# A two-layer decoder megakernel on one core: weight preparation reordered, one row chunk made full, keys moved to VectorE, a new instruction order

## What is computed

```python
x = _layernorm(x + _L0_attn_ref(x, ...))          # l0: 16 heads, rotary latents of 32, causal softmax
x = _layernorm(x + _L0_xattn_ref(ctx, x, ...))    # x0: q @ (k^T v), no softmax, own norm inside
x = _layernorm(x + _L0_ffn_ref(x, ...))           # f0: 256 -> 704 -> 256, FP4 blocks of 16, silu(gate) * up
x = _layernorm(x + _L1_attn_ref(x, ...))          # l1: causal softmax plus a second, softmax-free branch
x = _layernorm(x + _L1_xattn_ref(x, ctx, ...))    # x1: masked cross attention, then 256 -> 1024 -> 256
x = _layernorm(x + _L1_ffn_ref(x, ...))           # f1: 256 -> 256, FP6 blocks of 32
```

## Time and profile before

| | us |
|---|---|
| median of 3 runs | 1065.53 |
| lowest, highest | 1062.94, 1068.25 |
| the profiled execution, its own time | 1070.73 |
| span of its instructions | 1068.9 |

### The profile page before, as it was taken

The page is one execution under the profiler, slowest core; times in us unless marked ns, Lnnn a source line. Parts: engine busy times, 40 slices in busy tenths (PEclk is TensorE's granted clock), DMA queues, the critical chain, the costliest instruction groups (busy, mean ns, idle before and its releaser), DMA issues.

```text
span 1068.9 us, 29911 instructions
## 1 busy us (share of the span) xinstructions
PE 896.8 (84%) x12078; PEld 692.8 (65%) x12078; DVE 742.0 (69%) x1804; ACT 641.6 (60%) x1867; POOL 348.1 (33%) x604
## 2 busy tenths in 40 slices
PE   2665688999999898989999999999998989887853
PEld 2444466777767676767676776767776766665643
DVE  4956384869686876868686868687777878674342
ACT  1244457586767667585848675766767585836341
POOL 2752121333242323333243423242323333322121
PEclk7868899999999999999999999999999999988776
DMA  9102000000100100010101010000001000000000
GB/s 339 67 2 84 14 2 22 2 14 7 32 5 6 31 2 24 2 29 2 28 3 28 3 27 3 7 24 2 20 2 42 6 8 9 8 6 6 6 6 6
DMA packets 24440, 24.90 MB, mean 23 GB/s; under 512 B 2304, under 2 KB 22640, under 8 KB 24176
## 3 DMA queue, kind: packets, MB, share of 16 engines
q1 hardware_dynamic: 24304, 22.98, 6.9%
HBM read 18.80 MB, written 2.10 MB: 20 GB/s over the span
## 4 chain that ended last, share of the span: by engine, by line
PE 47%; DVE 19%; ACT 15%; DMA 8%; POOL 5%; issue 4%; SPq 2%; DVEq 0%; POOLq 0%; ACTq 0%
PE bank L1175 26%; PE s_tile L1175 13%; DMA out<-x_ 5%; ACT probT L648 5%; PE bank L1287 4%; ACT prob L710 3%; PE bank L1376 3%; POOL rstd L563 3%; DVE rope_ L964 2%; ACT x_ L757 2%; DVE stats L923 2%; DVE y_ L947 2%; DVE y_ L950 2%; DVE y_ L936 2%; DVE ma_ L1101 2%
## 5 line engine op out<-in xcount | busy, mean ns | idle before, releaser
L710 ACT ACTIVATE prob<-s_tile,low 128x128 f32<-128x128 f32 x768 | 218.9, 407 | 20.0 <-DVE low L977 19.9
L561 POOL TENSOR_TENSOR var_eps<-mean_var,rsq 128x1 f32<-128x1 f32 x144 | 32.3, 224 | 503.5 <-DVE mean_var L925 503.5
L972 DVE TENSOR_REDUCE peak<-s_tile 128x4 f32<-128x512 f32 x192 | 123.0, 682 | 31.5 <-PE s_tile L1175 31.4
L648 ACT ACTIVATE probT<-bank 128x512 f32<-128x512 f32 x192 | 100.0, 596 | 22.5 <-PE bank L1376 22.5
L757 ACT ACTIVATE x_<-y_,shift,rstd 128x256 f32<-128x256 f32 x96 | 58.0, 604 | 90.6 <-POOL shift L569 84.0
L563 POOL TENSOR_TENSOR rstd<-var_eps,rsq 128x1 f32<-128x1 f32 x144 | 87.7, 609 | 11.3
L648 ACT ACTIVATE xt_<-bank 128x256 f32<-128x256 f32 x128 | 50.1, 403 | 67.5 <-PE bank L1287 67.5
L1376 PE MATMUL bank<-cst,prob 32*128 32x32 f32 x3072 | 63.9, 229 | 15.7 <-ACT prob L710 9.5
L1376 PEld LDWEIGHTS bank<-cst,prob 32*128 32x128 f32 x3072 | 56.6, 143 | 30.3 <-ACT prob L710 14.8
L1175 PEld LDWEIGHTS bank<-xt_,w 128*128 128x128 f32 x512 | 62.5, 200 | 4.0 <-ACT xt_ L648 0.9
L923 DVE BATCH_NORM_STATS2 stats<-y_ 128x6 f32<-128x256 f32 x144 | 61.6, 427 | 5.0
(11 more groups left out here) (195 smaller groups left out, 2072.5 us busy)
## 6 DMA issues: line engine op xcount, KB each, us to landing
...
w<-in_gate_up SPq DMA_DIRECT2D x2, 512.0 KB, 9.1
```

The costliest lines, as they stand in the source:

```text
L561: pool.tensor_tensor(var_eps[:, b:b + 1], mean_var[:, b, 1:2], rsq[:, 0:1], ALU.add) .then_inc(eps_in, 1)
L648: emptied(act.activation(dst, src, ACT.Copy), i, key)
L710: ins = act.activation(prob[:, r, c * P:(c + 1) * P], bank[r][:, c * P:(c + 1) * P], ACT.Exp, scale=SCALES[layer], bias=low[:, b, h:h + 1])
L972: dve.tensor_reduce(peak[:, b, 4 * r:4 * r + 4], rows4(src[:, :]), AX_X, ALU.max)\
```

## The change

It does five things. First, SP loads up0 ahead of everything, up1 and up2 early, and cproj ahead of rows. Second, DVE quantizes up0 before its small setup instructions, which are now a stage of their own (`columns`); up0 is also rounded and dequantized on DVE (`round_up0`, three instructions), so POOL prepares five pieces, not six. The waits for the `rows` load move from the front of the queues to the first instructions that read it, and two memsets shrink. Third, the down projection's last chunk takes rows 576 to 703, a full 128, of which the first 64 meet zeros in `w_dn` (one memset on POOL). Fourth, `ka_` is made by one DVE instruction in `l1_project`, with a single semaphore `pairs_done`, in place of the two on ACT. Fifth, all of START, SLOTS and BANKS are new.

```diff
+            load_blocks_of("up0", gate_rows[:, 0:4, :])
             load("blocks", blk, blocks)
...
+            load_blocks_of("up1", gate_rows[:, 4:8, :])
             for b in range(2):
...
+            load_blocks_of("up2", gate_rows[:, 8:11, :])
+            load("cproj", w_cproj[:, :, :], by_rows(cproj))
             load("rows", rowt[:, :], rows.broadcast_to([P, rows.shape[1]]))
...
+            pool.memset(w_dn[0:TAIL, FK - 1, :], 0.0).then_inc(cleared, 1)
...
-                for e in range(2):
-                    ins = act.activation(ka_[:, b % 2, 2 * e:2 * e + 2, :], th2(b), ACT.Identity,
-                                         scale=col["halfmask"][:, e:e + 1], bias=col["halfmask"][:, e:e + 1])
-                ins.then_inc(ka_done, 1)
...
+            def round_up0(i, b):
+                src, block_ = sources["up0"], FP4["block"]
+                dve.wait_ge(quant_w, W_STEPS)
+                for n, op in enumerate((ALU.add, ALU.subtract)):
+                    dve.tensor_tensor(src, src, w_powers[:, 0, 0:src.shape[1]], op).then_inc(rounded_up0, 1)
+                    dve.wait_ge(rounded_up0, n + 1)
+                blocks_ = src.rearrange("p (a k) -> p a k", k=block_)
+                dve.tensor_tensor(blocks_, blocks_, long(q_scale[:, 0, 0:src.shape[1] // block_], block_), ALU.mult)\
+                    .then_inc(rounded_up0, 1)
...
                 dve.scalar_tensor_tensor(out=qa(b), in0=q_[:, b, 0:2, :], scalar=0.02,
-                                         in1=q_[:, b, 0:2, :], op0=ALU.mult, op1=ALU.min).then_inc(qa_done, 1)
+                                         in1=q_[:, b, 0:2, :], op0=ALU.mult, op1=ALU.min)
+                dve.scalar_tensor_tensor(out=ka_[:, b % 2, :, :].rearrange("p (e c) t -> p e (c t)", e=2),
+                                         in0=wide(th2(b).rearrange("p c t -> p (c t)"), 2), scalar=1.0,
+                                         in1=long(col["halfmask"], 2 * P), op0=ALU.add, op1=ALU.mult)\
+                    .then_inc(pairs_done, 1)
...
-                            ins = pe.transpose(dst[0:size, (2 * s + a) * P:(2 * s + a + 1) * P],
-                                               sources[f"down{a}"][:, c * P:c * P + size], ident)
+                            ins = pe.transpose(dst[:, (2 * s + a) * P:(2 * s + a + 1) * P],
+                                               sources[f"down{a}"][:, start:start + P], ident)
...
-    SP=dict(f0_down=0, l0_project=1470, l1_turn_x=1472, x1_mask=3502, x1_scores=5524, f1_norm=7555),
+    SP=dict(x1_mask=0, l0_project=1, f0_down=132, l1_turn_x=2178, x1_scores=4262, f1_norm=8320),
```

More of the change, by code:

```diff
@@ L69 @@
 SLOTS = dict(
[L70 to L80, removed]
@@ L81 @@
-    DVE=dict(v_bias=0, quant_up0=1, quant_up1=2925, quant_up2=5410, cproj_bias=6068, wo_bias=7509, x0_kv=60784,
-        l0_rope=61208, quant_down0=61396, x0_mix=61729, l0_scores=61899, l0_peaks=61986, quant_down1=62324,
-        quant_last=62657, l0_back=62675, l0_out=62726, x0_attend=63179, x1_mask=63207, x0_affine=63215,
-        f0_quant=63361, f0_scale=63473, f0_level=63578, f0_gate=64121, f0_gate2=64301, h_quant=64309,
-        h_scale=64467, h_level=64471, f0_down=64596, l1_scores=64799, l1_project=64806, l1_peaks=64977,
-        x1_keys=65225, l1_back=65465, l1_ma=65470, l1_below=65480, l1_ma_back=65621, l1_out=66056,
-        x1_peaks=66577, x1_scores=66594, x1_back=67078, x1_out=67590, x1_affine1=67807, x1_down=68581,
-        x1_affine2=68654, f1_quant=68777, f1_scale=68820, f1_level=68847, f1_out=69393),
@@ L105 @@
-BANKS = {"p_g": 7, "p_qk0": 5, "p_qk1": 7, "p_v": 4, "l0_project.qk": 7, "l0_v.v": 4, "l0_lat.s0": 0,
[7 rows of a table removed]
+    PE=dict(v_bias=0, l0_project=450, cproj_bias=1468, x0_kv=1943, turn_up0=1968, turn_up1=2195, l0_lat=2355,
+        l0_latent=2698, l0_scores=2738, l0_v=2817, x0_mix=3069, wo_bias=3106, l0_mix0=3107, l0_mix2=3129,
+        l0_mix1=3137, l0_mix3=3213, l0_value=3415, turn_up2=3462, l0_back=3617, l0_turn=3702, l0_out=3758,
+        x0_turn_x=4053, x0_project=4114, x0_attend=4270, turn_down1=4530, turn_last=4808, f0_turn_x=4982,
+        f0_up=5054, f0_up2=5067, f0_turn_h=5376, f0_turn_h2=5387, f0_down=5393, f0_down2=5402, l1_turn_x=5751,
+        l1_project=5830, l1_scores=6094, x1_keys=6372, l1_mix0=6440, l1_mix2=6448, l1_mix1=6457, l1_mix3=6501,
+        l1_value=6560, l1_back=6633, l1_ma=6666, l1_ma_value=6870, l1_ma_back=6945, l1_turn=7059, l1_out=7115,
+        x1_turn_x=7223, x1_project=7262, x1_scores=7464, x1_values=7655, x1_mix0=7953, x1_mix1=8016,
+        x1_mix2=8039, x1_mix3=8103, x1_value=8226, x1_back=8360, x1_turn=8683, x1_out=8885, x1_turn_h=9171,
+        x1_up=9255, x1_up2=9265, x1_down=9325, x1_down2=9513, f1_turn_x=10436, f1_out=10721),
@@ new lines @@
+    DVE=dict(quant_up0=0, columns=1618, v_bias=2325, quant_up1=2923, round_up0=4481, cproj_bias=7227,
+        quant_up2=7608, x0_kv=66429, l0_rope=66720, quant_down0=66861, l0_peaks=66992, l0_scores=67029,
+        wo_bias=67114, x0_mix=67151, quant_down1=67215, quant_last=67304, l0_back=67708, l0_out=68124,
+        x1_mask=68505, x0_attend=68654, x0_affine=68787, f0_quant=68887, f0_scale=68995, f0_level=69006,
+        f0_gate=69182, f0_gate2=69209, h_quant=69210, h_scale=69430, h_level=69497, f0_down=69718,
+        l1_scores=70289, l1_peaks=70588, l1_project=70589, x1_keys=70808, l1_back=70914, l1_ma=70927,
+        l1_below=70928, l1_ma_back=71105, l1_out=71183, x1_scores=71748, x1_peaks=71864, x1_back=72817,
+        x1_out=73055, x1_affine1=73220, x1_down=73682, x1_affine2=73862, f1_quant=73963, f1_scale=74206,
+        f1_level=74349, f1_out=75058),
```

141 lines of the change are left out of this document (72 added, 69 removed), and 24 rows, old and new, of the table BANKS.

## The result

The changed kernel took 1036.38 us (median of 4 runs, 1035.96 to 1038.29) against 1066.89 us for the kernel before (4 runs, 1062.94 to 1068.87): a ratio of 0.972, 95% interval 0.969 to 0.976, so 30 us or 2.8% less. 1052 was forecast, with a range of 1036 to 1068: the side was right, the gain twice what the sum gave. The profiled execution took 1038.29 us, its span 1036.5; before, 1070.73 and 1068.9.

The account below looks back on a forecast made before the run. PE was taken as the bound in the steady part, DVE's weight work at the start. The terms and +0.4 for x0_mix.1 summed to -13.8 us, giving 1052 from the plain median 1065.53; range 1036 to 1068.

Parts of the forecast that it names:

- Term A: Fill, DVE's start: up0 loaded and quantized first brings l0_back.0 to 61.7 in place of 66.45, -4.8 us.
- The blocking: Fill: round_up0 on DVE is held up beside POOL's additions for up1, 4.7 us more, bounds 0 and 4.8.
- the two short waits: Fill: DVE waits twice for PE's bias products, 0.7 us each by estimate, 1.4 us.
- Term B: Fill, PE's order: turn_down1 and x0_kv.1 move behind tile 0's x0, so x0_turn_x.0 comes sooner, -3.2 us.
- Term C: Fill: SP issues tile 2's xtin load ahead of its wait for the weights' transposes; f0_up.0 at 84.1, a further -5.7 us.
- Term D: Steady part, some 13 tiles: the new order's gains and losses give about -0.15 us per tile, -2 us in all.
- Rival 1: Steady part: the order is better than seen, PE's gaps fall 1 us per tile; 1028 to 1043, chance 0.17.
- Term E: Drain: x1_affine2.14 stands ahead of x1_peaks.15 on DVE, where PE and ACT wait for the peaks, +1.5 us.
- Rival 3: Steady part: xtin's load behind DVE's x1_mask makes PE wait 1.5 to 1.7 us per tile; 1068 to 1076, chance 0.10.

Follow-up runs that it names:

- after_up0_pool: The changed kernel with up0 rounded and multiplied on POOL again and DVE's three round_up0 instructions gone: 1035.91 us, ratio 0.969.
- edits_alone: The changed kernel with the old START, SLOTS and BANKS, apart from the first places of DVE's queue: 1059.54 us, ratio 0.994.
- after_down2_early: The changed kernel with PE's old places for the second half of x1's down product and f0's hidden-row transposes: 1035.16 us, ratio 0.970.
- after_ka_act: The changed kernel with the matching keys (ka) back on ACT in two instructions and gone from DVE: 1035.07 us, ratio 0.968.
- after_tail: The changed kernel with the 64-row last chunk of the down projection put back: 1036.21 us, ratio 0.972.
- before_l1_ma_early: The kernel before with l1_value, l1_back and l1_ma in their new places on PE, l1_back, l1_ma, l1_below ahead of f0_quant on DVE: 1076.35 us.
- before_full: The kernel before with only the last chunk of the down projection made a full one: 1062.09 us, ratio 0.997.
- after_down1_early: The changed kernel with turn_down1 put back ahead of x0_turn_x.0 on PE, its copies with it on ACT: 1037.23 us, ratio 0.972.
- order_alone: The kernel before with the new START, SLOTS and BANKS and none of the other edits: 1045.85 us, ratio 0.980.
- after_l1_back_late: The changed kernel with l1_value, l1_back and l1_ma in later places on PE, behind x1_turn and the next projection: 1061.71 us, ratio 0.995.

## Why the prediction was right or wrong

The range held, by 0.4 us: 1036.38 against a lower end of 1036. That is luck, as the kernel's own runs, 1035.96 to 1038.29, lie on both sides of it, and the sum itself, 1052, was 16 us off. The prediction's own sign of being wrong, a pace per tile that differs by over 0.5 us, came: 56.3 against 57.2.

**Term A** held in its sum: -4.8 measured -5.7 at `l0_back.0`. The blocking was priced at 4.7 over 3.7 unhindered and came to 4.1; the two short waits of 1.4 us did not come, and 1.4 us of stretching that the term had left out did (the scaling of `rowt`). Its account of what goes when POOL has no up0 was incomplete: by after_up0_pool, where up0 is rounded is worth nothing (1035.91 against 1036.38), because POOL's work would then fall on the setup. What the term did not say is that its gain needs the others: in edits_alone it is down to 0.6 us at `f0_up.0`, lost in the wait for xtin.

**Term B** came out as -3.3 for -3.2, with a false reading and some luck in the number. `x0_kv.1` did not move, and the norm chain hid it; up to 2.5 of the 3.3 us are the low clock of the profile before, since the same queue took 7.2 us at full clock where that profile had 9.6.

**Term C** came out as -5.7 for -5.7. That f0_up.0 and not the load would be late next, and that the gain reaches the end, was right: undoing C alone gave back 10.2 us at `f0_up.0` and 8.6 at the end. That this is more than 5.7 shows again that the fill's terms are no separate prices; the sum was right because all of them were made at once.

**Term D** is the step that failed, though the range covered it. It read the two queues move by move and summed the waits it could name, -0.15 us per tile; measured were -1.1 over twelve tiles, with the slow stretch in them, and -1.6 over tiles 8 to 14. Its listed items do not add up to the -0.15 unless ACT's lighter queue stands for some 0.8 us of gain. Of its items:
- the gap ahead of f0_down shrank by 0.43, as said, but is worth nothing (after_down2_early);
- ACT's 1.10 us for ka, with DVE's 0.7 for it, is worth nothing (after_ka_act);
- the last down chunk was put at nothing: it saves PE 0.2 us per tile (after_tail), which does not show at the end;
- l1_scores was to lose 0.5 and lost 0.03: ACT's two exponentials ahead of l1_project (500.57 to 503.02 in one tile) ran beside PE's own l1_project (500.42 to 503.36);
- l1_back was to lose 0.2 and did;
- missed altogether were the waits that went ahead of l0_v (0.30), x1_turn (0.23), l1_turn_x (0.18), x1_out (0.17) and x0_turn_x (0.13), and those that came, ahead of l1_value (0.43) and x1_turn_h (0.25). Missed too was that a stage of PE that no longer follows a wait is also shorter itself: with the full chunk 0.8 us per tile in all.

But for l1_turn_x, the missed waits were each small in the profile before, under 0.35 us, and the term looked at the two largest. Its bound of -1.5 per tile, a third of the gaps, covers the -1.1 and just misses the -1.6. **Rival 1** named this case: PE's gaps fall by 1 us per tile. The argument against it, that the two largest waits end on chains that are not shorter, was wrong for `f0_down` (0.47 to 0.04), right in the main for `l1_turn_x` (0.99 to 0.81), and beside the point, since the other gaps gave the gain. Its chance of 0.17 was too small, and so 1036.4 lay at the edge of the range.

**Term E**: the instructions of x1_affine2.14 do stand ahead of the second half of x1_peaks.15,

```profile
988.81 0.48 DVE L958 SCALAR_TENSOR_TENSOR y_<-y_,mean_var,rowt 128x256 f32<-128x256 f32 x1
...
990.41 1.26 DVE L983 TENSOR_REDUCE peak<-s_tile 128x4 f32<-128x512 f32 x2
```

which is 1.60 us by these rows. The drain as a whole was 2.7 us shorter, and that goes with the clock. From the end of tile 15's l0 scores to the last instruction, by the clock granted there:

| order | granted clock: drain in us |
|---|---|
| old (before, edits_alone, before_l1_ma_early, before_full) | 0.84: 175.6; 0.86: 173.1; 0.87: 173.2; 0.89: 169.9 |
| new (after_up0_pool, after_down1_early, changed kernel, after_tail, order_alone) | 0.86: 173.6; 0.86: 174.0; 0.88: 172.9; 0.89: 171.3; 0.89: 171.4 |

In either order the drain is shorter at the higher clock, and at like clock it is 0.5 to 1.5 us longer in the new order (2.0 and 2.7 in after_l1_back_late and after_down2_early, 175.1 and 175.8 at 0.86). So the term's sign and about its size are borne out, as far as single executions show it.

**Rival 3** was rightly put low. In the changed kernel DVE's mask, the load behind it and the projection that needs it are

```profile
509.21 0.21 DVE L1131 TENSOR_SCALAR mask_f<-mask_i 128x128 f32<-128x128 int32 x1
```

```profile
510.30 0.73 SPq L486 DMA_DIRECT2D xtin<-in_xT  x1
```

```profile
521.10 2.05 PE L1192 MATMUL bank<-xtin,w_qk 128*128 128x128 f32 x16
```

With the 7.3 us of flight of the earlier trace rows the load lands at 517.6, 3.5 us early, where up to 4.7 was forecast, and PE's projection shows no wait for it.
